# A graph network's gathers: index lists kept in SBUF and copied into place by ACT, in place of loads by SP

## The reference

```
h = max(layernorm(x), 0);  x = x + L0(h, edges, edge_attr_2)    # two spline convolutions, mean over edges
h = max(layernorm(x), 0);  x = x + L1(h, edges)                 # GCN: segment_sum(norm * h[src], dst)
h = max(layernorm(x), 0);  x = x + L2(h, src, dst, edge_attr_32)# messages by an MLP, summed, update MLP
h = max(layernorm(x), 0);  x = x + L3(h, src, dst, edge_attr_16)# three layers with batch norm between

# spline convolution:
xw  = einsum('ni,kio->nko', h, W)          # 25 products for each node
msg = einsum('es,eso->eo', basis, xw[src[:, None], widx])
agg = segment_sum(msg, dst)
# L3's layer:
m = concatenate([x[dst], x[src], ea]) @ W.T + b;  relu(segment_sum(m, dst))
```

## Time and profile before

| | |
|---|---|
| median of 3 runs | 20082.57 us (20068.84 to 20102.87) |
| the profiled execution | 20154.05 us, its span 20152.2 us |
| PE | 8383.3 us busy (42%), 34014 instructions |
| DVE | 4749.9 us (24%), 7949 |
| ACT | 1130.3 us (6%), 2610 |
| POOL | 11020.9 us (55%), 11663 |
| DMA traffic | 1320.35 MB, mean 66 GB/s |

### The profile page before, as it was taken

The page is one execution under the profiler, slowest core; times in us unless marked ns, Lnnn a source line. Parts: engine busy times, 40 slices in busy tenths (PEclk is TensorE's granted clock), DMA queues, the critical chain, the costliest instruction groups (busy, mean ns, idle before and its releaser), DMA issues.

```text
span 20152.2 us, 144869 instructions
## 1 busy us (share of the span) xinstructions
PE 8383.3 (42%) x34014; PEld 7106.5 (35%) x34014; DVE 4749.9 (24%) x7949; ACT 1130.3 (6%) x2610; POOL 11020.9 (55%) x11663
## 2 busy tenths in 40 slices
PE   7655555344443333334444443333323333333333
PEld 4333444233333333334444433333323333223333
DVE  4333333233332111112323221111121111211111
ACT  2101111000000000000111100000000000000000
POOL 0355555455555665655555556555545555465655
PEclk9877777677776555556666665555555555555555
DMA  4444444333332111113333321111111111111111
GB/s 194 151 127 143 143 145 145 99 94 95 95 95 61 26 29 29 29 36 88 88 86 87 87 64 24 23 24 23 23 25 23 23 23 23 26 24 25 26 25 24
DMA packets 1013136, 1320.35 MB, mean 66 GB/s; under 512 B 546589, under 2 KB 704574, under 8 KB 987470
## 3 DMA queue, kind: packets, MB, share of 16 engines
q0 software_dynamic: 426240, 764.57, 15.7%
q1 hardware_dynamic: 586830, 555.05, 8.6%
HBM read 970.98 MB, written 347.67 MB: 65 GB/s over the span
## 4 chain that ended last, share of the span: by engine, by line
another core or an unknown queue 57%; PE 18%; issue 13%; DVE 7%; DMA 1%; SPq 1%; DVEq 1%; ACT 1%; ACTq 0%; POOL 0%; POOLq 0%
PE PS L770 10%; PE PS L690 4%; DVE BIG L1376 2%; DVE OH L1356 1%; PE PS L699 1%; DMA AG<-acc 1%; PE PS L803 1%; PE PS L764 1%; DVE BIG L1383 1%; DVE BIG L1391 0%; DVE XC L1224 0%; PE PS L677 0%; ACT STG L971 0%; SPq L485 0%
## 5 line engine op out<-in xcount | busy, mean ns | idle before, releaser
L770 PE MATMUL PS<-BIG,OH 128*128 128x64 f32 (+3 forms) x23310 | 5742.5, 428 | 3488.2 <-DVE OH L1356 1837.9
L611 POOL DMA_INDIRECT BIG<-t_mp,IDX x4995 | 4715.1, 944 | 3512.2 <-issue 1714.7
L770 PEld LDWEIGHTS PS<-BIG,OH 128*128 128x128 f32 x23310 | 5083.9, 296 | 4025.7 <-DVE OH L1356 1884.2
L611 POOL DMA_INDIRECT BIG<-t_cell,IDX x3330 | 3151.1, 946 | 3150.7 <-issue 1795.2
L764 PE MATMUL PS<-STG,CARRY 128*128 128x64 f32 (+3 forms) x1554 | 566.5, 463 | 6424.0 <-ACT STG L971 4910.6
L1356 DVE TENSOR_TENSOR OH<-REL,PS 128x640 f32<-128x640 f32 x2331 | 1885.2, 816 | 3815.8 <-remote 3125.4
L764 PEld LDWEIGHTS PS<-STG,CARRY 128*128 128x128 f32 x1554 | 352.6, 282 | 6598.9 <-ACT STG L971 4889.6
L611 POOL DMA_INDIRECT BIG<-t_p,IDX x1665 | 1579.6, 949 | 1335.4 <-DMA IDX<-in_src 574.3
L611 POOL DMA_INDIRECT BIG<-t_gcn,IDX x1665 | 1573.9, 945 | 1092.9 <-DMA IDX<-in_src 596.6
L803 PE MATMUL PS<-BIG 128*128 128x128 f32 x3330 | 593.7, 341 | 1101.7 <-DVE BIG L1383 969.9
L1354 DVE TENSOR_SCALAR CARRY<-PS,DELTA 128x128 f32<-128x128 f32 x777 | 270.7, 348 | 3185.7 <-remote 2261.7
(11 more groups left out here) (150 smaller groups left out, 3317.2 us busy)
## 6 DMA issues: line engine op xcount, KB each, us to landing
t_cell<-BIG SPq DMA_DIRECT2D x198, 1280.0 KB, 4.5
BIG<-in_dst_row SPq DMA_DIRECT2D x333, 240.0 KB
BIG<-t_mp,IDX POOLq DMA_INDIRECT x4995
BIG<-t_cell,IDX POOLq DMA_INDIRECT x3330
BIG<-t_gcn,IDX POOLq DMA_INDIRECT x1665
BIG<-t_p,IDX POOLq DMA_INDIRECT x1665
BIG<-in_ef SPq DMA_DIRECT2D x333, 80.0 KB
BIG<-t_q SPq DMA_DIRECT2D x333, 48.0 KB
```

The source lines that it names most:

```text
L611: nc.gpsimd.indirect_dma_start(to[:, j, :], None, table, bass.IndirectOffsetOnAxis(ap=IDX[:, s // CHUNKS, at:at + 1], axis=0)).then_inc(ga ...
L770: last = nc.tensor.matmul(WIN[:, 0:out_w], OH[:, s % CHUNKS, j * P:(j + 1) * P], src[:, j, :], start=False, stop=(s % CHUNKS == CHUNKS - 1 ...
```

## The change

Two tiles are added in SBUF, each 128 x 1665: CELLS with the whole list of the spline passes, written there by DVE at the start, and SRCS with the sources, loaded at the start. ACT copies fifteen columns of one of them into a slot of IDX: three lists at the start of a pass, and then list g+3 right behind the staging of window g (copy_list), counted by the one semaphore list_ready, for which POOL waits. SP no longer loads lists and no longer waits for gathers; it keeps coefficients, edge attributes, the mlp operands, and the stores of windows and node rows. The spline table's list is still stored to cell_idx, which only the path for unsorted input reads. The "sum" passes on ACT now have their first and last unit written out, since the last unit copies no list.

```diff
+        CELLS = sb("CELLS", [P, z.tiles], I32)
+        SRCS = sb("SRCS", [P, z.tiles], I32)
...
-        idx_in = [sem(f"idx_in{s}") for s in range(UNIT)]
+        list_ready, idx_in = sem("list_ready"), sem("idx_in")
...  SP
-            todo = [(REL[:, :].bitcast(I32), t["dst"]), (SLOTI, t["src"]),
+            todo = [(REL[:, :].bitcast(I32), t["dst"]), (SLOTI, t["src"]), (SRCS[:, :], t["src"]),
-            sp.dma_start(cell_idx, SLOTF.bitcast(I32)).then_inc(sem("cell_stored"), 16)
+            sp.dma_start(cell_idx, CELLS[:, :]).then_inc(sem("cell_stored"), 16)
...
-                def load_list(g, to):
-                    sp.dma_start(IDX[:, to, :], lists[:, bass.ds(g * TILES, TILES)]).then_inc(idx_in[to], 16)
-                    if kind == "spline":
-                        sp.dma_start(COEF[:, to, :], coef_d[:, bass.ds(g * TILES * 4, TILES * 4)]
-                                     ).then_inc(coef_in[to], 16)
+                def load_coefficients(g, to):
+                    sp.dma_start(COEF[:, to, :], coef_d[:, bass.ds(g * TILES * 4, TILES * 4)]
+                                 ).then_inc(coef_in[to], 16)
...
-                    if c == 0 and not (last and gi + AHEAD >= UNIT):
+                    if kind == "spline" and c == 0 and not (last and gi + AHEAD >= UNIT):
                         if not (first and gi == 0):
-                            before = [(s - CHUNKS + q) % SLOTS for q in range(CHUNKS)]
-                            for q in before:
-                                sp.wait_ge(gathered[q], 16 * CT * (ub + u + (1 if gi > 0 else 0)))
-                                hold(sp)
-                            if kind == "spline":
-                                sp.wait_ge(coef_copied, gb + g)
-                                hold(sp)
+                            sp.wait_ge(coef_copied, gb + g)
+                            hold(sp)
...
-                        load_list(g + AHEAD, (gi + AHEAD) % UNIT)
+                        load_coefficients(g + AHEAD, (gi + AHEAD) % UNIT)
...  POOL
-                            pool.wait_ge(idx_in[s // CHUNKS], 16 * (ub + u + 1))
+                            pool.wait_ge(list_ready, gb + u * UNIT + s // CHUNKS + 1)
...  ACT
+                lists = CELLS if kind == "spline" else SRCS
+                def copy_list(g, to):
+
+                    nc.scalar.activation(IDX[:, to, :], lists[:, bass.ds(g * TILES, TILES)], copy
+                                         ).then_inc(list_ready, 1)
...
                     if c == CHUNKS - 1:
                         stage_window(g)
+                        if not last:
+                            copy_list(g + UNIT, s // CHUNKS)
...  ACT, mlp pass
-                        stage_window(u * UNIT + s // CHUNKS - 1)
+                        g = u * UNIT + s // CHUNKS - 1
+                        stage_window(g)
+                        if not (last and s > 0):
+                            copy_list(g + UNIT, (s // CHUNKS - 1) % UNIT)
...
+                for g in range(UNIT):
+                    copy_list(g, g)
...  DVE, at the start
-            link(v.tensor_copy(SLOTF.bitcast(I32), flat))
+            link(v.tensor_copy(CELLS[:, :], flat))
```

More of the change, by code:

```diff
@@ L461, in fast_pass @@
                 kind, table, width, acc = passes[n]
-                gb, ub = z.groups * n, z.units * n
-                lists = cell_idx if kind == "spline" else t["src"]
-                def load_list(g, to):
-                    sp.dma_start(IDX[:, to, :], lists[:, bass.ds(g * TILES, TILES)]).then_inc(idx_in[to], 16)
-                    if kind == "spline":
-                        sp.dma_start(COEF[:, to, :], coef_d[:, bass.ds(g * TILES * 4, TILES * 4)]
-                                     ).then_inc(coef_in[to], 16)
+                gb = z.groups * n
+                def load_coefficients(g, to):
+                    sp.dma_start(COEF[:, to, :], coef_d[:, bass.ds(g * TILES * 4, TILES * 4)]
+                                 ).then_inc(coef_in[to], 16)
                     if n == 0:
@@ L488, in body @@
                 def body(u, s, first, last):
-                    c = s % CHUNKS
-                    g = u * UNIT + s // CHUNKS
-                    gi = s // CHUNKS
-                    if c == 0 and not (last and gi + AHEAD >= UNIT):
+                    c, gi = s % CHUNKS, s // CHUNKS
+                    g = u * UNIT + gi
+                    if kind == "spline" and c == 0 and not (last and gi + AHEAD >= UNIT):
                         if not (first and gi == 0):
-                            before = [(s - CHUNKS + q) % SLOTS for q in range(CHUNKS)]
-                            for q in before:
-                                sp.wait_ge(gathered[q], 16 * CT * (ub + u + (1 if gi > 0 else 0)))
-                                hold(sp)
-                            if kind == "spline":
-                                sp.wait_ge(coef_copied, gb + g)
-                                hold(sp)
+                            sp.wait_ge(coef_copied, gb + g)
+                            hold(sp)
                             if n == 0:
@@ L519, in node @@
                     node_slot(n, s, k, CREDIT_STORE + 16 * (gb + (k + z.lag) * UNIT - 1))
-                for g in range(AHEAD):
-                    load_list(g, g)
+                if kind == "spline":
+                    for g in range(AHEAD):
+                        load_coefficients(g, g)
                 end_phase(n)
@@ L549, in body @@
                         hold(sp)
-                    sp.dma_start(IDX[:, 0, 0:1], lists[:, bass.ds(i, 1)]).then_inc(idx_in[0], 16)
+                    sp.dma_start(IDX[:, 0, 0:1], lists[:, bass.ds(i, 1)]).then_inc(idx_in, 16)
                     if not first:
@@ L599, in fast_pass @@
                 kind, table, width, acc = passes[n]
-                cb, ub = z.chunks * n, z.units * n
+                cb, gb = z.chunks * n, z.groups * n
                 with pool.Fori(0, z.units) as u:
@@ L630, in body @@
                 def body(i, first):
-                    pool.wait_ge(idx_in[0], 16 * (tb + i + 1))
+                    pool.wait_ge(idx_in, 16 * (tb + i + 1))
                     if not first:
@@ L1000, in fast_pass @@
                     stage_window(z.groups - 1)
-                elif n == 0:
-                    copy_attributes(0, 0, 0)
+                else:
+                    if n == 0:
+                        copy_attributes(0, 0, 0)
                     edged_units(act, body, node)
-                else:
-                    all_units(act, body, node)
                 tail_steps(node)
```

## The result

The changed kernel takes 19367.6 us (median of 3 runs, 19343.21 to 19377.25) against 20082.57 us: a ratio of 0.964 with an interval of 0.9619 to 0.9662. That is 715 us less, where 1230 us were forecast; the time lies in the range, about halfway between the forecast (18,850 us) and the rival of late completions (19,900 us).

The account below looks back on a forecast made before the run. POOL's gathers were taken to bound the kernel, with idle time waiting for lists. Gains 943 + 426 - 3 = 1366 us, a tenth off: 1230; 20,154.1 - 1230 - 71.5 gives 18,850 us, range 17,900 to 20,050.

Parts of the forecast that it names:

- late completions: Rival: PE's late completions bound the loop, most saved idle time returns as other stalls; 19,900 us, chance 0.15.
- What bounds the kernel: POOL's 11655 gathers, 1.25 us each, 14,570 us of 20,152; only idle time at a group's start can be shortened.
- The new way: From a window's staging to POOL's start: window copy 0.22, list copy 0.21, POOL's own 0.30, together 0.7 us, before 4.99.
- 45.8% of the list waits goes: Share from four stalls, 23.24 of 42.87 us remaining; 943 us of 2059 in gcn and the three last passes.
- A tenth off for catching up: Shorter stalls move staging forward by less than POOL, so the gain of 1366 us was cut to 1230.
- A sign that failed: If right, POOL's wait ended by ACT's list copy would be about half of 2990 us outside the mlp pass.
- The spline passes: Two passes with 930.5 us of list waits; the 45.8% share gives 426 us gained.
- The mlp pass at nothing: Its 574.3 us of list waits are off the path; POOL stands 9.4 us longer at a start, covered by its lead.
- The slower rival: Stricter start condition in the mlp pass costs up to 9.4 us for each of 110 groups; 20,940 us, chance 0.12.
- the side sum: Gain of 1350 us instead of 1366 if an ACTIVATE takes the skill page's 0.31 us, 0.1 us more per stall.
- Hidden anyway: Rival: the transfer is already hidden, the saved way comes back as later staging; 20,080 us, chance 0.05.
- Staging leaves the path: Rival: SP, free of lists, lets windows be staged sooner; list waits outside mlp go altogether; 17,090 us, chance 0.08.

Follow-up runs that it names:

- the pair on chip A: Changed kernel with ACT loading lists by DMA instead of copying, 0.992; changed kernel with SP also loading every list into an unread tile, 0.9741; both against the kernel before.

## Why the prediction was right, and where its size was off

- **What bounds the kernel: right.** Gathers stay at 0.945 us and 1.25 us apart, and the whole gain is idle time ahead of them (787.2 of 786.4 us).
- **The new way, 0.7 us assumed: 1.22 us measured.** The copy lasts what was said (0.22 us in the stall above, 0.21 on average), but POOL starts 0.88 us after it ends (0.86 to 0.95 us in 458 waits); the 0.30 us that lie between two gathers don't hold for a start after a wait. Over the some 225 stalls of the four sum passes that is 117 us less.
- **The step that failed in size: 45.8% of the list waits goes.** In the gcn and t_mp passes 561.6 us of idle time went of the 943 predicted, 27% of 2059. The percentage came from four stalls, one of which, with its window staged before POOL ran out, gave 7.61 of the 19.6 us saved. In the sixth pass only 4 of 56 stalls are such. Without it the three others give 12.02 of 34.96 us, 34%; with the longer way 30%.
- **A tenth off for catching up: a quarter was given back** in the sixth pass. The way is 4.07 us shorter, a stall 3.1 us. The mechanism was named, its size was not taken from anything. It isn't one size either: in the pair on chip A the t_mp passes give back hardly anything of 1.5 us and the gcn pass all of it.
- **A sign that failed.** The list wait outside the mlp pass was to be about half of 2990 us; it is 3576.4 - 797.0 = 2779 us. The matmul-ended waits, 874 us, which the sum left alone, now end with the copy as well, and the staging comes later. By list waits alone this would read as "late completions"; the 787 us of idle time that went say that it is in between.
- **The spline passes: 208.8 us for 426.** By the gathers' starts the first pass became 54 us shorter, the second 159. In the first, 65 of 102 stalls had their window staged before POOL ran out, the best case for the change by my own rule; after it the staging comes behind POOL's end in each of the 72 stalls of over 1.5 us, 8.2 us on average, and most is given back. There "late completions", the second rival, is what happened.
- **The mlp pass at nothing: right, but not as told.** It is 18 us shorter (8708.9 to 11557.2 us), one engine waited for a gather there, once, for 2.3 us, and the experiment with a longer way left it alone. But POOL doesn't stand 9.4 us longer at a start: its idle time there is 1318.6 us where it was 1335.4, and the staging comes 6.1 us after its last gather where it came 13.2. What was to be POOL's loss came back as an earlier staging. The slower rival's condition was there (POOL now starts behind the staging), its price was not.
- **The start at 3 us: 1.4 us**, from the first gather's start, 724.4 and 725.8 us.
- **ACT 163 us busier: 79 us.** The copy starts 0.12 us after the staging starts, so half of it lies under the staging's 0.22 us. Nothing hung on it.
- **Two slips without effect.** With ACT's copy 0.1 us longer, the four stalls of 42.87 us save 0.4 us less; of 2990 us that is 28, so the side sum would have been 1338 and not 1350 us. And the 0.70 us of the earlier trace rows is the time of SP's issuing instruction, not of the transfer.
- **"Hidden anyway"** had 0.05. It is wrong for the chip of the forecast, and right for chips B and C, whose ratio is 0.9994. The Trainium skill ("DMA: Bandwidth & Descriptors", Rules for kernel authors) has it that an early issue hides a DMA's fixed cost; chip C's trace agrees, with lists issued at POOL's pace, two groups of 18.8 us ahead less the 6 us by which they follow a group's last gather. The first chip's doesn't, since SP's issue is held up by a late window. The chances were given as if a kernel had one time. No row of one trace could tell of the other chips.
- **"Staging leaves the path"**: no; in the gcn, t_mp and spline passes staging is later against POOL than before. Moving the copy ahead of it, which takes the staging out of the list's chain, brought 0.9569 on chip A; by its waits it brought no more because slots are freed late as well.

What stays open is why completions are late on some chips. PE's busy time (8383.3 and 8683.4 us), the gathers' duration, the granted clock and DMA times as of t_cell's stores (4.5 us) don't show it.

## What to carry to other kernels

Split a wait at its releaser's releaser before pricing it: only the part behind the last late event can be saved, and a quarter of even that may come back, or, as in the gcn pass of the pair on chip A, all of it. Take the share from all stalls of each pass, counted by whether the late event fell before or after the engine ran dry, and not from a few in a row. And where the releaser's idle time reads "remote" and its input had been ready for tens of microseconds, the stall may belong to the chip: run both kernels on another one before believing or paying for the gain.

## What the runs showed of the hardware

- The kernel before took 20082.57, 19857.43, 15830.34 and 15852.22 us in four measurements, each within 0.4% in itself (the 25 runs on B within 0.11%). The last three are of three different chips. The instructions' durations are the same; what differs is how soon other engines go on after PE: 21.5 us or 0.13 us after a group's last matmul. Lateness comes and goes within a pass: of the 111 windows of the sixth pass in the kernel before's first trace, 39 are staged over 10 us after their last matmul's end, up to 42.8 us, and 64 within 1 us; on chip C none takes longer than 0.42 us. It isn't the granted clock: in each of the four sum passes it is 0.50, the lower level of 1.2 GHz, in both traces.
- On the first chip ACT stages 5.5 us after POOL stops in the stall above, and in the sixth pass 6.2 us after on average; with a fifth of the matmuls on chip A there are 17 stalls in the gcn pass for 54. On chip C, with all matmuls and all gathers, completions are prompt. On a late chip that points to POOL's gathers and PE's instruction count together. It is not shown: the experiment with fewer gathers ran on prompt chips only.
- From the end of ACT's copy to the start of the gather that waits for it 0.88 us pass (median of 458 waits), an ACT copy of 128x15 takes 0.20 to 0.24 us, and with a 128x15 load issued by ACT in its place 2.71 us pass from the staging to the gather.
